# Slab loads issued back to back and earlier on one DMA queue, and convolution folds moved one token earlier

## The reference, cut to what matters

```python
out = lax.conv_general_dilated(x, weight, window_strides=(1,), padding=[(4, 4)], feature_group_count=4, ...)
y = out + ctx[:, :, None] + bias[None, :, None]

def fake_quant(t, axis):
    s = jnp.maximum(jnp.max(jnp.abs(t), axis=axis, keepdims=True) / 127.0, 1e-08)
    return jnp.clip(jnp.round(t / s), -128.0, 127.0) * s
gate = fake_quant(y, -1) @ fake_quant(w_gate, 1).T      # 512 -> 1376
up   = fake_quant(y, -1) @ fake_quant(w_up, 1).T
h    = silu(gate) * up
return x + fake_quant(h, -1) @ fake_quant(w_down, 1).T  # 1376 -> 512
```

## Time and profile before

| what | value |
|---|---|
| time, median of 3 runs | 301.11 us (300.82 to 302.56) |
| the profiled execution | 301.11 us, its span 299.3 us |
| TensorE matmul busy | 286.2 us, 96% of the span |
| VectorE busy | 250.5 us, 84% |
| GpSimd busy | 199.2 us, 67% |
| ScalarE busy | 194.3 us, 65% |
| DMA queue of SyncE | 51.10 MB, 62.8% of the 16 engines' span |
| granted TensorE clock | 1.0 in all of the span |

### The profile page before, as it was taken

How to read it: one execution, slowest core, us unless ns; L and a number is a source line. 1 busy time by engine, 2 the same in 40 slices (tenths; PEclk the granted TensorE clock), 3 DMA queues, 4 the chain that set the end, 5 groups by cost and what they waited for, 6 DMA issues and landing times.

```text
span 299.3 us, 4766 instructions
## 1 busy us (share of the span) xinstructions
PE 286.2 (96%) x1641; PEld 168.8 (56%) x1641; DVE 250.5 (84%) x407; ACT 194.3 (65%) x229; POOL 199.2 (67%) x207
## 2 busy tenths in 40 slices
PE   6996999997999999999999999999999999999995
PEld 6995666743555555555444567655444444444443
DVE  3879769999799897988988878898988889889863
ACT  1268699997377666654778835354788767667640
POOL 1586869998177767653788836442778887666653
PEclk9999999999999999999999999999999999999999
DMA  7999742559955569844269993426355874433336
GB/s 272 418 423 368 298 67 52 115 114 239 251 173 151 141 190 212 230 150 120 85 172 294 209 232 96 115 52 91 102 153 153 170 187 118 106 89 94 83 93 216
DMA packets 80535, 51.59 MB, mean 172 GB/s; under 512 B 69536, under 2 KB 70048, under 8 KB 79616
## 3 DMA queue, kind: packets, MB, share of 16 engines
q1 hardware_dynamic: 80224, 51.10, 62.8%
q10 hardware_dynamic: 288, 0.20, 0.3%
HBM read 25.99 MB, written 8.39 MB: 115 GB/s over the span
## 4 chain that ended last, share of the span: by engine, by line
PE 68%; POOL 8%; ACT 7%; DVE 6%; DMA 5%; issue 4%; SPq 1%; DVEq 0%; POOLq 0%
PE bank L953 37%; PE bank L970 17%; PE bank L840 12%; DMA slab<-x_blocks 4%; POOL sg_mem L471 4%; POOL hq_mem L423 2%; DVE h_max L749 2%; DVE h_mem L743 2%; DVE sg_mem L733 1%; DMA hq_mem<-hq_mem 1%; ACT y_mem L519 1%; POOL y_mem L450 1%; ACT sg_mem L575 1%; ACT hq_mem L587 1%; PE bank L1013 1%
## 5 line engine op out<-in xcount | busy, mean ns | idle before, releaser
L471 POOL TENSOR_TENSOR sg_mem<-sg_mem,gu_scale_row 128x512 f32<-128x512 f32 (+1 forms) x96 | 111.2, 1161 | 74.2 <-ACT sg_mem L575 74.2
L953 PE MATMUL bank<-wgu_t,xq_mem 128*128 128x512 bf16 (+1 forms) x768 | 155.4, 357 | 2.9 <-DVE h_mem L743 2.5
L953 PEld LDWEIGHTS bank<-wgu_t,xq_mem 128*128 128x128 bf16 x768 | 74.1, 99 | 74.7 <-DVE h_mem L743 7.8
L575 ACT ACTIVATE sg_mem<-sg_mem,x_scale 128x512 f32<-128x512 f32 (+1 forms) x96 | 63.6, 673 | 48.9 <-DVE sg_mem L733 48.6
L970 PE MATMUL bank<-wd_t,hq_mem 128*128 128x512 bf16 (+1 forms) x341 | 78.2, 379 | 0.0
L733 DVE TENSOR_TENSOR sg_mem<-bank,gu_scale_row 128x512 f32<-128x512 f32 (+1 forms) x96 | 60.3, 628 | 19.1 <-PE bank L953 19.1
L743 DVE SCALAR_TENSOR_TENSOR h_mem<-bank,x_scale,sg_mem 128x512 f32<-128x512 f32 (+1 forms) x96 | 66.3, 692 | 11.1 <-POOL sg_mem L471 9.8
L580 ACT ACTIVATE h_mem<-h_mem,h_inv 128x1376 f32<-128x1376 f32 x32 | 46.1, 1442 | 30.2 <-DVE h_inv L625 30.2
L970 PEld LDWEIGHTS bank<-wd_t,hq_mem 128*128 128x128 bf16 (+1 forms) x341 | 33.3, 98 | 40.2 <-issue 0.3
L840 PEld LDWEIGHTS bank<-toeplitz,slab 128*128 128x128 f32 x320 | 48.1, 191 | 5.0 <-DMA slab<-x_blocks 1.4
L749 DVE TENSOR_REDUCE h_max<-h_mem 128x1 f32<-128x1376 f32 x32 | 50.5, 1577 | 0.0
(11 more groups left out here) (59 smaller groups left out, 132.0 us busy)
## 6 DMA issues: line engine op xcount, KB each, us to landing
xo_mem<-x SPq DMA_DIRECT2D x24, 256.0 KB, 3.0
out<-xo_mem SPq DMA_DIRECT2D x24, 256.0 KB, 2.2
slab<-x_blocks SPq DMA_DIRECT2D x3, 1088.0 KB, 6.8
hq_mem<-w_gate_up SPq DMA_DIRECT2D x6, 512.0 KB, 7.3
slab<-x_blocks SPq DMA_DIRECT2D x3, 1024.0 KB, 5.7
slab<-w_down SPq DMA_DIRECT2D x3, 688.0 KB, 9.4
h_mem<-w_gate_up SPq DMA_DIRECT2D x4, 512.0 KB, 14.6
slab<-x SPq DMA_DIRECT2D x1, 2048.0 KB, 9.4
```

Source lines behind the costliest of these rows:

```text
L471: pool.tensor_tensor(s, s, gu_scale_row[:, 1, at:at + n], ALU.mult).then_inc(silu_scaled, 1)
L575: act.activation(s, s, ACT.Silu, scale=x_scale[:, i:i + 1]).then_inc(silu_done, 1)
L953: last = pe.matmul(bank[n % 2][:, 0:cols], xq_t[:, g, k, P * c:P * (c + 1)], wgu_t[:, m, k, at:at + cols], start=(k == 0), stop=(k == KT - 1))
```

## The change

Two tables of the hand-written order are changed, and no operation is added or removed.

First, `FOLDS_AT`: fold 11 moves from token 4 to token 3, behind fold 9. Fold 13 moves from token 5 to token 4. Fold 15, and with it `group_top(1)`, `group_scale(1)` and `group_inverse(1)`, stays in token 5 and stands there alone.

Second, the slab loads on SyncE: both halves of slab 2 are issued at i = 4 (before: at 4 and 6), and both halves of slab 3 at i = 5, ahead of the first residual loads (before: at 9 and 11).

```diff
-        FOLDS_AT = {3: [9], 4: [11], 5: [13, 15]}
+        FOLDS_AT = {3: [9, 11], 4: [13], 5: [15]}
...
             for i in range(TILES + 1):
                 for o in down_at(i - 2):
                     turn_w_down(o)
-                if i in (4, 6):
-                    load_slab(2, i // 2 - 2)
-                if i in (9, 11):
-                    load_slab(3, (i - 9) // 2)
+                if i == 4:
+                    load_slab(2, 0)
+                    load_slab(2, 1)
                 if i == 5:
+                    load_slab(3, 0)
+                    load_slab(3, 1)
 
                     for b in range(WDQ_BUFS):
                         sp.wait_ge(wd_turned[b], 16 * KT // WDQ_BUFS)
```

## The result

The changed kernel takes 303.99 us (median of 4 runs, 303.77 to 305.59) against 300.97 us for the kernel before in the same job (300.72 to 302.56). The ratio is 1.0115, with a 95% interval from 1.0076 to 1.0156: 1% slower, clear of noise. The profiled execution took 303.64 us, with a span of 301.8. The result lists 16 executions of the changed kernel in all, from 303.52 to 307.07 us with a median of 304.25.

A forecast was written before the change was run, and what follows sets the result against it. TensorE, busy all 60.30 us from 75.0 to 135.3, was taken as the bound. A 2.2 us wait for yq 7 plus 0.5 for restarts gave 301.1 + 2.7 = 303.8 us, range 301.3 to 306.0.

The forecast's parts named there:

- A transpose behind a slab waits for it: SyncE's queue: three more slab halves, 8.2 us of bulk, delay yq 7's landing from 80.8 to 89.0.
- restart term: SyncE's queue: extra delay behind long bulk, since issue is not free; between 0 and about 1.5 us, taken as 0.5.
- TensorE's wait at token 7 sets the time: Token 7, wanted at 86.84: TensorE waits 2.2 us for yq 7, 2.7 with 0.5 for restarts.
- The wait to look for: Profile after: a TensorE idle row of 2 to 3.5 us at about token 7's first matmul, released by the transpose into xq_mem.
- The folds cost 0.3 us, covered by the slab: Tokens 3 to 5: VectorE's work slides 1.2 us; the slab's wait covers all but 0.3, not added to the 2.7.
- GpSimd's addition waits 1.6 us, under TensorE's wait: Token 0's residual addition at 84.58: residual 0 lands at 86.2, so GpSimd waits 1.6 us, hidden under TensorE's wait.
- Nothing is gained by the emptier queue later: Tokens 6, 9 and 11: TensorE waited for none of the slab halves taken away there, so nothing is won.
- yq 6 fits by 0.3 us: Token 6: yq 6 lands at 78.1 instead of 75.4, and the token begins at 78.43.
- The first (absorbed): Rival: the queue absorbs the bulk, yq 7 lands before 86.84, time 301.1 to 301.5 us; chance 0.16.
- The price per half slab of the second: Rival: bulk costs more than its rate, 4.7 us per half, 309 us; mild end 305.8; chance 0.14.
- The third: Rival: the folds decide, 1.2 us on top: 305.0 with the queue's cost, 302.3 without; chance 0.08.
- The rate of 392 GB/s: Measured from 71 to 73 us with only slab packets: three halves, 3.21 MB, take 8.2 us.

The follow-up runs named there:

- slab 2 pair: The kernel before with slab 2's second half issued right behind its first at i = 4, slab 3 and folds as before: 300.95 us, ratio 1.0001.
- slab 3 pair: The kernel before with both halves of slab 3 at i = 5 ahead of the residual loads, slab 2 and folds as before: 301.89 us, ratio 1.0024.
- its copy without that loss: The changed kernel with 20 idle matmuls of 128 columns in TensorE's wait in token 4: 304.38 us, ratio 1.0118.
- slab 3 behind the residuals: The changed kernel with folds as before and both slab 3 halves behind the four residual loads, still ahead of yq 7's transpose: 305.91 us, ratio 1.0154.

## Why the prediction was right, and where it was not

- **A transpose behind a slab waits for it.** Right, and the step on which all hangs. yq 7 landed at 89.4 where the sum had 89.0 and a restart term of 0.5. That is 8.6 us later for 3.21 MB against the 8.2 + 0.5 of the sum. The sum counted only bulk ahead of the transpose; in the trace 4.1 of the 8.6 us passed before yq 7 was even issued, since the issue of hq 3 began 1.2 us later and held SyncE 1.3 us longer, and two more slab issues (1.1 us) stood ahead. It landed at 83.9 to 84.5 behind the slab 2 pair, 86.9 behind the slab 3 pair, and 89.4 to 90.2 behind both, whether the residuals stood before or after them.
- **TensorE's wait at token 7 sets the time.** Right for the place and for the size of the delay (2.5 us in the trace, 2.7 forecast), and the rule that earlier delays are not added to it held: the changed kernel starts token 7 at 89.38 with 1.6 us lost in token 4, and its copy without that loss at 90.24. The wait to look for, 2 to 3.5 us, is only 0.85 in the changed kernel, since TensorE comes to the transfer late; with the loads alone it is 2.78.
- **The folds cost 0.3 us, covered by the slab.** Right at the full clock (300.70 to 301.09 us, no loss), and wrong in its steps. With the folds alone TensorE's row behind the wait in token 4 starts at 69.05 instead of 68.22, 0.8 us later and not 1.2, and the wait itself grew by 0.5. Nor did the slab land at 74.9: with the folds alone its first half landed 6.3 us after its issue at 68.09, at 74.4, so what covered the slide was in part a slab that came sooner. The busy share of a 27 us stretch was too coarse a view to price a slide of one operation. And in five of twelve runs the granted clock fell behind the longer wait and took 1.7 us, of which the prediction has no word.
- **What the prediction missed: a wait can cost more than itself.** It priced the idle time and assumed full speed behind it. For the loads alone it would have said 303.8, and five runs of six took 305.4 and more. In the profiled execution of the change the number came out all the same, because the fall lay ahead of token 7, in the shadow of the late transfer. So it did in four of the ten executions with a fall, and six more had none; the other six took 1.2 to 3.3 us more than the forecast. The number was partly luck: in the profiled execution one loss lay under the other.
- **GpSimd's addition waits 1.6 us, under TensorE's wait.** Right: 1.43 us, and without it nothing changed.
- **Nothing is gained by the emptier queue later.** Right: TensorE's three waits beyond 100 us are the same in the two traces, and the spans stay apart by the 2.5 us of token 7.
- **yq 6 fits by 0.3 us.** Off by about 1 us: with the loads alone it came 0.58 us late, with the slab 2 pair 0.77. With the loads alone it landed at 78.5 instead of 78.1, and token 6 wanted it at 78.0 instead of 78.4, since the slab's first half came sooner than the prediction had it. That gain is also why the late yq 6 cost next to nothing.
- **The rivals.** The first (absorbed) is what each pair does alone, nearly. The price per half slab of the second did not come. The third had 302.3 for the folds alone, and five of twelve runs took 302.4 to 302.8, but because the clock fell; that the slab landed sooner cost nothing in the seven at the full clock.

The rate of 392 GB/s was near enough. In the changed kernel the stretch in which mostly slab packets run moves more still:

```profile
80.00:83.00 3.00, 3.00 (x16) 1.35 (x15) 2.90 (x7) 1.22 (x2) 0.94 (x1) 1.00 1.02 411
```

411 GB/s for three microseconds is above the 358 that the Trainium skill gives for a core's load from HBM ("DMA: Bandwidth & Descriptors", section "Where 436 GB/s comes from"). The same section also cites a measured load at 425 GB/s, and that is the side on which the trace falls. The delay of yq 7 alone would not decide it: 8.6 us lies between the 8.2 of the one rate and the 9.0 of the other.

## What to carry to other kernels

Before a bulk transfer is moved forward in a queue, list what it is moved past, and the time each of those has in hand. Here the delays in a queue added up, so that two moves which were nearly free one by one cost 2.7 us together. And a wait on TensorE should be priced with what may come behind it: here waits of 2.0 to 3.1 us were followed, in 18 of 31 runs, by a stretch at half clock that cost 1.5 to 2.0 us more. Look at the granted clock of the stretch behind it, run the kernel often enough to see whether the times fall in two groups, and if they do, try some idle matmuls in the wait before anything is rearranged.

## What the runs showed of the hardware

- The granted clock fell to 0.50 (1.2 GHz) behind some waits of TensorE and not behind others. By the longest wait of each kernel's profiled execution, these are the runs with a mean of 0.994: behind 1.5 us (the kernel before in all four jobs, and the five kernels without idle matmuls whose waits are no longer) 7 runs of 150, behind 2.03 us (folds alone) 5 of 12, behind 2.57 us (the changed kernel with idle matmuls in token 4) 3 of 6, behind 2.78 us (loads alone) 5 of 6, behind 3.06 us (slab 3 behind the residuals) 5 of 7. With a part of the wait filled by idle matmuls it was 1 of 11 (0.91 us left), 0 of 12 (0.41 us left) and 0 of 4 (1.15 us left). The fillers hardly moved what stands behind them (the next row starts at 68.78 instead of 69.05, 68.48 instead of 68.42, and 89.74 instead of 89.91), so a mere shift in time is an unlikely cause, though none was tried by itself. Why one run falls and the next does not, the runs do not show.
- A stretch at half clock lasted 3.4 us in the changed kernel (70.4 to 73.8) and cost 1.5 to 1.7 us in the rows: the 12 matmuls of 512 columns behind it took 4.26 us instead of 2.76, the 16 of token 4 5.05 instead of 3.36. In whole runs it was 1.7 us with the folds alone (by averages) and 1.9 to 2.0 with the loads (by medians, in two kernels). In the kernel before, such runs were only 0.6 to 1.2 us above their median; no profile shows where theirs fell.
- The first half of slab 2 landed 6.8 us after its issue in the kernel before and in the one with slab 3 alone moved, but after 5.8 to 6.2 us wherever its second half was issued right behind it. I had expected the same or longer. It is not the second half that does it, or not alone: with the folds alone moved, without and with the idle matmuls, it landed after 6.3 and 6.0 us, and there the issue of hq 3 had come at 72.13 and 71.86 instead of 71.12. Which of the two counts was not tested.
- A DMA transpose can hold the issuing queue: that of an hq tile took 1.36 us as a rule, 1.7 to 3.5 us behind one half slab, and 4.7 to 6.5 us behind two. The commands behind it start later by that much, so that the time to landing alone does not show all of the delay.
